# Attention scores in a fused attention and expert layer: from one matmul over 128 output columns to four over 32

## The reference

```python
x = L0_attn_x                                   # 8 x 1024 x 256, float32
x = x + _layernorm(_L0_attn_ref(_layernorm(x), Wq, Wk, Wv, Wo))
x = x + _layernorm(_L0_ffn_ref(_layernorm(x), router_weight, router_bias, gate_up_proj, ...))
# _L0_attn_ref: 16 heads of 16 columns each
score = jnp.einsum('bhnd,bhmd->bhnm', q, k) * scale
score = jnp.where(causal, score, -jnp.inf)
attn = jax.nn.softmax(score, axis=-1)
out = jnp.einsum('bhnm,bhmd->bhnd', attn, v)
# _L0_ffn_ref: 8 experts of width 512, the two best for each token
```

## Time and profile before

| what | value |
|---|---|
| median of the runs | 2070.23 us |
| the profiled execution, its span | 2073.1 us |
| instructions in it | 50022 |
| attention stage | up to about 1260 us |
| expert stage and last normalisation | from about 1260 us |

### The profile page before, as it was taken

How to read it: one execution, slowest core, us unless ns; L and a number is a source line. 1 busy time by engine, 2 the same in 40 slices (tenths; PEclk the granted TensorE clock), 3 DMA queues, 4 the chain that set the end, 5 groups by cost and what they waited for, 6 DMA issues and landing times.

```text
span 2073.1 us, 50022 instructions
## 1 busy us (share of the span) xinstructions
PE 1952.6 (94%) x13552; PEld 1293.3 (62%) x13553; DVE 1587.0 (77%) x5413; ACT 1329.5 (64%) x3387; POOL 934.1 (45%) x1439
## 2 busy tenths in 40 slices
PE   6799999999999999999999989999999999999980
PEld 5344444444444444444434338999999999999980
DVE  3877788888888888888888756778777777777767
ACT  4277777777777777777777675565444544544436
POOL 4333344445555646546555464554333333333335
PEclk9799999999999999999999999999999999999995
DMA  6633546455455554544536457988989999998858
GB/s 204 196 113 123 180 141 208 150 178 187 140 166 159 156 167 139 181 150 143 170 117 211 137 175 217 264 253 246 271 253 259 264 260 264 263 257 256 232 136 327
DMA packets 257526, 410.10 MB, mean 198 GB/s; under 512 B 36912, under 2 KB 194352, under 8 KB 250160
## 3 DMA queue, kind: packets, MB, share of 16 engines
q1 hardware_dynamic: 217856, 363.46, 54.6%
q0 software_dynamic: 29680, 35.41, 9.6%
q10 hardware_dynamic: 9792, 8.93, 1.4%
HBM read 284.83 MB, written 122.28 MB: 196 GB/s over the span
## 4 chain that ended last, share of the span: by engine, by line
PE 85%; DVE 7%; issue 3%; ACT 2%; DMA 2%; POOL 1%; SPq 0%; DVEq 0%; ACTq 0%; POOLq 0%
PE ps_s L1511 17%; PE ps_o L1395 13%; PE ps_s L1357 12%; PE ps_e L1376 10%; PE ps_e L1511 6%; PE ps_e L1528 6%; PE ps_o L1528 5%; PE ps_w L1427 5%; PE ps_w L1442 3%; PE ps_w L1458 3%; DVE arena L768 2%; PE ps_e L1521 1%; PE ps_w L1482 1%; DVE space L128 1%; DVE cmax L771 1%
## 5 line engine op out<-in xcount | busy, mean ns | idle before, releaser
L1141 ACT ACTIVATE arena<-ps_e 128x512 f32<-128x512 f32 (+3 forms) x1536 | 692.0, 493 | 277.5 <-PE ps_e L1376 266.4
L768 DVE CUSTOM_DVE_ANT_0 arena<-ps_s,c 128x128 bf16<-128x128 f32 (+3 forms) x1024 | 478.8, 481 | 84.7 <-PE ps_s L1357 80.3
L1357 PE MATMUL ps_s<-arena 96*128 96x512 bf16 (+3 forms) x1536 | 492.0, 336 | 18.8 <-DVE mrow L782 7.5
L1376 PE MATMUL ps_e<-arena 98*128 98x512 bf16 (+3 forms) x1536 | 483.3, 329 | 3.1 <-ACT arena L1141 2.0
L771 DVE TENSOR_REDUCE cmax<-ps_s 128x1 f32<-128x512 f32 x512 | 351.7, 687 | 125.0 <-PE ps_s L1357 116.3
L1357 PEld LDWEIGHTS ps_s<-arena 96*128 96x128 bf16 x1536 | 152.5, 101 | 350.7 <-DVE cmax L768 90.0
L1395 PE MATMUL ps_o<-arena 128*32 128x512 f32 (+3 forms) x3072 | 328.2, 499 | 6.1 <-ACT ot L1155 3.7
L662 POOL TENSOR_SCALAR_AFFINE_SELECT arena<-arena 128x512 f32<-128x512 f32 x256 | 162.5, 635 | 284.0 <-ACT arena L1141 283.7
L645 POOL DMA_INDIRECT acc<-blank,place_now x135 | 212.3, 1573 | 142.6 <-POOL place_now L638 60.8
L1511 PE MATMUL ps_s<-arena 128*128 128x128 f32 x2192 | 268.0, 275 | 0.1
L1511 PEld LDWEIGHTS ps_s<-arena 128*128 128x128 f32 x2192 | 262.0, 192 | 6.0 <-issue 1.1
(11 more groups left out here) (187 smaller groups left out, 3038.6 us busy)
## 6 DMA issues: line engine op xcount, KB each, us to landing
arena<-in_gate_up SPq DMA_DIRECT2D x91, 1024.0 KB
arena<-qk_parts SPq DMA_DIRECT2D x384, 128.0 KB, 3.0
c_h<-in_gate_up SPq DMA_DIRECT2D x44, 1024.0 KB
qk_parts<-space SPq DMA_DIRECT2D x120, 192.0 KB
d_xin<-xs SPq DMA_DIRECT2D x136, 130.5 KB
arena<-v_aug SPq DMA_DIRECT2D x32, 512.0 KB, 4.9
o_t<-ot SPq DMA_DIRECT2D x64, 256.0 KB, 2.0
v_aug<-space SPq DMA_DIRECT2D x28, 512.0 KB, 3.9
```

The lines of the kernel that those rows point to most:

```text
L768: dve.tensor_tensor_reduce(summed[:, m % RJ, 0:w], ps_s[:, m % RS, 0:w], after[:, HALF - w:HALF], 1.0, LOWEST, ALU.add, ALU.max, dst).then ...
L1141: act.activation(pw[:, n % RP, 0:w], ps_e[:, n % RE, 0:w], ACT.Exp, scale=SCALE).then_inc(e_done, 1)
L1357: pe.matmul(ps_s[:, m % RS, 0:w], qs[0:ROWS, slot, i * P:(i + 1) * P], ks[0:ROWS, slot, k0:k0 + w], start=True, stop=True).then_inc(s_scor ...
L1376: pe.matmul(ps_e[:, n % RE, 0:w], ks[0:ROWS_M, slot, j * P:(j + 1) * P], qs[0:ROWS_M, slot, q0:q0 + w], start=True, stop=True).then_inc(e_ ...
```

## The change

Both score matmuls, L1357 and L1376, are cut along the stationary operand. Where one instruction took 128 columns of it and wrote 128 partitions of PSUM, four instructions take 32 columns each and write 32 partitions each, of the same bank, with the same moved operand. The waits stand before the first of the four and the semaphore is counted up by the last. Sizes, buffers, the order of the pieces and all other engines' programs stay.

```diff
-                pe.matmul(ps_s[:, m % RS, 0:w], qs[0:ROWS, slot, i * P:(i + 1) * P], ks[0:ROWS, slot, k0:k0 + w],
-                          start=True, stop=True).then_inc(s_scores, 1)
+                for at in range(0, P, QUAD):
+                    last = pe.matmul(ps_s[at:at + QUAD, m % RS, 0:w], qs[0:ROWS, slot, i * P + at:i * P + at + QUAD], ks[0:ROWS, slot, k0:k0 + w],
+                                     start=True, stop=True)
+                last.then_inc(s_scores, 1)
...
-                pe.matmul(ps_e[:, n % RE, 0:w], ks[0:ROWS_M, slot, j * P:(j + 1) * P], qs[0:ROWS_M, slot, q0:q0 + w],
-                          start=True, stop=True).then_inc(e_scores, 1)
+                for at in range(0, P, QUAD):
+                    last = pe.matmul(ps_e[at:at + QUAD, n % RE, 0:w], ks[0:ROWS_M, slot, j * P + at:j * P + at + QUAD], qs[0:ROWS_M, slot, q0:q0 + w],
+                                     start=True, stop=True)
+                last.then_inc(e_scores, 1)
```

## The result

The changed kernel takes 2088.02 us, the median of two runs (2087.77 to 2088.26), against 2070.23: the ratio is 1.0086, with a 95% interval of 1.0067 to 1.0105. It is slower by 18 us, where 4 us less was forecast. The profiled execution has a span of 2086.6 us, 13.5 more than the 2073.1 before. The traces can account for these 13.5; for the other 4 us between the medians there is no trace.

What follows compares the result with a forecast made beforehand. TensorE's own stream was taken to set the attention stage's pace. -126.7 + 113.4 + 5 + 6 = -2.3 us, up to 5 less, called -4: 2069.1 us profiled, 2066 median; eight-in-ten range 2034 to 2108.

Steps and rivals of the forecast that it cites:

- The pieces: Score pieces: 3072 become 12288 matmuls with a load each, taken at +0.002 us a piece, or 6 us.
- A: Narrow score matmuls: loads go out one behind another, so pieces slow down; 2116 us, or 2152 at worst; chance 0.14.
- B: Attention stage: TensorE isn't fed matmuls and loads fast enough; a 5% shortage gives 2121 us; chance 0.06.
- D: Score pieces: the four narrow matmuls queue and run one by one; 1475 us more, 3541; chance 0.02.
- E: Score pieces of 128 columns: a floor under each matmul start costs 28 us, giving 2094; chance 0.07.
- What goes and what comes: TensorE's stream: 126.7 us removed around `weigh` and transposes, 113.4 us added at 362 full stretches.
- The 0.24 per stretch: Each of 362 full stretches: two passages of 0.10, 0.02 stagger, 0.02 first narrow load; 86.9 us in all.
- stagger: Ahead of each full stretch: 0.02 us until the fourth of four narrow matmuls is under way.
- Rival C: Full stretches: first load goes out ahead of the passage, or passage is cheaper; 32.5 us unpaid, 2034; chance 0.10.
- The free passage: First `values` piece of a pair: its wait for L791 covers the passage, 6 us less over 27 places.
- what stays hidden behind other engines: Attention stage: 5 of 13 us gained in quads 25 to 30 lost to VectorE waits; elsewhere nothing late.
- By region: Quads 0 to 3 gain about 1.3 us each, 25 to 30 about 2.2; fully loaded quads go 3.96 to 4.07.

Runs made afterwards that it cites:

- x1: Changed kernel with the maxima taken over only the first half of each piece's columns: 2077.48 us, ratio 1.0023.
- x2: Kernel before the change with the maxima taken over only the first half of each piece's columns: 2057.05 us, ratio 0.9928.
- x9: Changed kernel with maxima, and exponentials from the 48th on, over half of each piece's columns: 2063.89 us, ratio 0.9966.
- x10: Kernel before the change with maxima, and exponentials from the 48th on, over half of each piece's columns: 2046.46 us, ratio 0.9879.
- z3: Changed kernel; VectorE's copy reads a constant, the piece behind `weigh` doesn't wait for it, subtraction of the maxima left out: 2084.53 us, ratio 1.0062.
- z4: Kernel before the change; VectorE's copy reads a constant, the piece behind `weigh` doesn't wait, subtraction of the maxima left out: 2067.53 us, ratio 0.9982.
- z2: Kernel before the change with the transpose of the maxima over 128 stationary columns, 112 of them zeros: 2053.79 us, ratio 0.9931.

## Why the prediction was wrong

- **The pieces.** I took +0.002 us each. The second half of `weigh` was the right row to judge by: spacing is 0.22, 0.11 and 0.06 us as before, so the 6 us that I added aren't there. Rivals A, B, D and E fell here, and that 2088 lies near E's 2094 is chance. The Trainium skill's page "TensorE: Matmul & The Clock Gate", section "Wait — 56ns, not 53.3ns?", has a floor of about 25 ns between starts, and its page "TensorEngine Tiling (Array Packing)", section "Restrictions", says that column tiling disables the fast load of weights. Either would have shown in pieces of 128 columns: four matmuls with four loads take 0.06 us in this trace, so the trace agrees with neither as a cost here. A narrow load has a mean of 96 ns for a quarter of the columns, a full one 101: slower for its columns, but hidden.
- **What goes and what comes.** Forecast: -126.7 + 113.4 + 6 = -7.3 us for TensorE's stream. Measured: -42.4 + 27.3 - 6.4 = -21.5. The sign and the kinds were right, and the prices of 0.10 for a passage and 0.10 for a first load held. The 0.24 per stretch was too high, since stagger and narrow load come to 0.02, not 0.04 (612.72 to 612.88 is 0.16 for 0.06), some 7 us over 362 stretches. The sum also had nothing for the transposes, whose 0.05 us run beside the next piece now, 6 us in all. Rival C fell: L1431 lasts 1.13.
- **The free passage.** "One place gets its passage free", 6 us. It did not: the idle time ahead of `values` (passage included) grew from 11.3 to 17.6 us over the same 25 places, since the chain that ends it grew by 0.23 us in each.
- **The step that failed** is "what stays hidden behind other engines": "Elsewhere nothing is late: VectorE and ScalarE wait for the scores", priced at 5 us. The waits grew by 35.1. I had read that TensorE hardly waits as proof that nothing else bounds it. That row only says that the others were just in time, with passages of 0.10 us standing where a hand-over needed them. And that ScalarE and VectorE wait for scores in total 133.0 and 58.6 us does not say that they have time to spare where TensorE needs them next.
- **By region.** Quads 0 to 3: forecast -1.3 us each, measured -0.1. Quads 5 to 24: forecast +0.1 each, measured +0.8. Quads 26 to 28: forecast -2.2, measured -0.2 each (97.2 to 96.7 us).
- **Theories.** VectorE's load alone (x1, x2), both engines' load (x9, x10), and the hand-over alone (z3, z4) each leave the gap. All together take 12 of 18 us. The rest stands in the quads 5 to 24. By the traces its places are the exponential piece that waits for ScalarE behind L1165 and L1249 and the chain through L1165 and L791; as its cause they are read, not shown.

## What to carry to other kernels

In these traces a passage between full and narrow stationary operands costs 0.10 us of TensorE's time, and the first load of weights behind it doesn't go ahead of it (0.10 us more for a full float32 one). Count passages in the order, for all work that shares TensorE, and not for the instructions that are changed. Making the smaller kind wide (here a transpose of 16 columns padded to 128) can save more than making the larger kind narrow: 17 us less in z2, 18 more in the change.

Where TensorE waits for almost nothing, and two other engines are busy for more than three quarters of the time (VectorE 492.51 and ScalarE 463.11 of 600 us here), don't count time taken out of its stream as gained until you know which wait comes next. Find the hand-overs that end just in time and ask which piece of the stream covers them. Easing one of them moved the wait to the next; it took all three to see what they cost.

## What the runs showed of the hardware that was not expected

Column strips of 32 work on their own. In the changed kernel the transpose of 16 columns starts at 633.93 and the next piece of four at 633.94: three of its matmuls start by 633.944 and the fourth at 633.992, behind the 0.05 us of the transpose, which so occupies one strip. Before, the same transpose held all of TensorE for 0.05 plus two passages. Four bfloat16 matmuls of 128 columns in four strips, each with a load, are through in 0.06 us (612.61 to 612.66), which is 7 ns an instruction.
